# Attention and expert layers on one core: 64 units in one sequence, one batch's side work beside the other's units

## The chip, the cores and the metric

The kernel runs on one core of a Trainium2 chip. The metric is the device time of one execution in microseconds (us); the median of three runs is the figure before. The data are float32; inside, some operands are kept in bfloat16 (bf16), often as a value split into two or three bf16 parts whose sum is the float32 value.

## The reference

Input x is 2 batches of 1024 tokens of 128 numbers. All is computed in float32. LN is a layer norm without weights.

```python
x = x + LN(attention_1(LN(x)))     # 16 heads of 8; a bias table added to the logits
z = LN(x)
z = z + attention_2(LN(z) * ln1_w + ln1_b)   # 16 heads, no bias, then times w_proj
z = z + experts(LN(z) * ln2_w + ln2_b)       # each token goes to the one expert of 8
x = x + LN(z)                                # with the largest gate logit
```

attention_1 has `logits = q k^T / sqrt(8) + bias[h, i - j]`, softmax over 1024 keys per batch and head, and its result is normed and added to x. attention_2 has the same 1024 x 1024 logits per batch and head, without a bias. An expert is 128 -> 512, gelu, -> 128.

## The kernel before, in words

**Units and stages.** One head of one batch is a unit (1024 x 1024 logits). Stage 0 (attention_1) has 32 units, stage 1 (attention_2) has 32. The order inside a stage is head by head, and batch 0 then batch 1 within a head. Each engine's program is written out by hand in this order; semaphores tie the engines together. No scheduler changes it.

**What a unit does.** Its logits are computed twice. First in 8 "A blocks" (128 queries x 1024 keys): PE writes a block with `scores_a` (L1147) into one of two PSUM slots `SA`, and DVE takes each query's maximum over it, in stage 0 with the bias table added on the way (`block_max`, L876), in stage 1 with a plain reduce (L879). Then POOL splits the 8 maxima into three bf16 parts (`split_maxima`, L598 to L603), PE transposes them (L1184), ACT copies them out (L724), and SP sends them through DRAM into three extra rows of q (`maxima_of`, L424 and L428). Second in 8 "kb steps" of 128 keys x 1024 queries: PE writes two halves with `scores_b` (L1200), in stage 0 adds the bias by `bias_b` (L1207) from a skewed bf16 table, ACT takes the exponential (L737), and PE multiplies by v with `weigh_v` (L1155), two steps behind. At kb 2 ACT copies the last unit's sums out (`evacuate`, L707), and SP stores them. Three PSUM banks `SB` hold the halves on their way to ACT.

**Interleaving.** PE runs the kb steps of unit u together with the A blocks of unit u + 2: `scores_b`, `scores_a`, `scores_b`, `scores_a`, then `bias_b`, then `weigh_v`. An A block waits until DVE is done with the block two before.

**Loads.** SP loads, per head, the head's q and k rows for both batches (`rows_of`, 10 DMAs of 2048-token rows, issued over two units; L395, L398, L400), the bias table of the head (`table_of`, two DMAs of 480 KB, L332) and the skewed table (`skew_of`, 378 KB, L338). POOL copies v of the head for both batches (`v_of`, L579).

**Around the stages.** Before stage 0: x is normed (`norm_stats` L796 and L799, `norm_apply` L804 to L810, ACT's share L665 and L669), transposed (L1092), projected to q, k, v (L1113, L1116, L1121), split into parts (ACT L676 to L685, DVE L843 and L847) and stored to DRAM (L371, L375). Between the stages, for both batches at once: the last sums are loaded back, turned to token order (`to_natural`, L1138 and L1141), divided (`natural`, L860 and L863), normed, added to x, normed twice more, transposed, projected, split, stored, and rows of the first head are loaded. `keep_warm` (L1086) issues 12 idle matmuls. After stage 1: the same turn and division, times w_proj (L1299), added (L941), normed, the gate (L1330), the sorting of tokens by expert, 23 tiles of experts with indirect DMAs by POOL (L642, L653), the last norm and the stores.

## Time and profile before

| what | value |
|---|---|
| median of 3 runs | 986.47 us (985.25 to 987.48) |
| the profiled execution's own time | 982.59 us |
| its span, first to last instruction | 980.9 us |
| mean granted TensorE clock | 0.923 |
| busy PE, DVE, ACT, POOL | 830.7, 750.7, 648.3, 136.7 us |
| by stretch: up to the first kb step of stage 0 | 72.66 us |
| units 0 to 29 of stage 0 | 381.08 us |
| the last two units of stage 0 (no A blocks beside them) | 24.76 us |
| between the stages | 72.84 us |
| first unit of stage 1, then the other 31 | 12.73 and 287.03 us |
| after stage 1 | 129.80 us |

PE, DVE, ACT, POOL are TensorE, VectorE, ScalarE and GpSimd; SP issues DMAs. PEld is PE's load of the stationary operand. A busy share is an average over stretches with different limits, so the stretches are read apart. A matmul of float32 operands has two records.

### The profile page before, as it was taken

How to read it: one execution, taken by the hardware profiler on the slowest of the kernel's cores; microseconds unless marked ns; L12 is line 12 of the kernel's file. 1: busy time of each engine (PE TensorE's matmuls, PEld its weight loads, DVE VectorE, ACT ScalarE, POOL GpSimd, SP SyncE). 2: the span in 40 equal slices, each digit the busy share in tenths (PEclk: the TensorE clock that was granted, in tenths of full speed). 3: DMA queues.
4: the chain of work that ended last, by engine and by line, in shares of the span. 5: the costliest groups of instructions: out<-in, count | busy, mean ns of one | idle time of the engine just before them, and what ended most of it. 6: DMA issues, size and time to landing. Idle time of an engine off the chain costs nothing.

```text
span 980.9 us, 22683 instructions
## 1 busy us (share of the span) xinstructions
PE 830.7 (85%) x9011; PEld 315.4 (32%) x9011; DVE 750.7 (77%) x1211; ACT 648.3 (66%) x1272; POOL 136.7 (14%) x376
## 2 busy tenths in 40 slices
PE   2449999999999999999735799999999999974770
PEld 1203333333333333333312122222222222354760
DVE  6477777777777777774297899999999999266544
ACT  5406777677777777777434499999999999710222
POOL 8100000000000000000010011011010110003772
PEclk9758999999999999999967599999999999975995
DMA  2654434444444443330005365322222121010123
GB/s 62 173 157 104 120 95 109 105 106 107 107 98 110 107 106 93 87 86 16 16 1 152 81 149 134 105 69 70 65 66 70 58 69 42 24 44 19 50 49 94
DMA packets 55609, 82.79 MB, mean 84 GB/s; under 512 B 12336, under 2 KB 42480, under 8 KB 55504
## 3 DMA queue, kind: packets, MB, share of 16 engines
q1 hardware_dynamic: 53648, 76.57, 29.6%
q0 software_dynamic: 1472, 3.02, 1.3%
q10 hardware_dynamic: 384, 1.76, 0.6%
q8 instruction: 71, 1.16, 0.5%
q14 instruction: 34, 0.28, 0.1%
HBM read 62.31 MB, written 19.01 MB: 83 GB/s over the span
## 4 chain that ended last, share of the span: by engine, by line
PE 65%; ACT 9%; DVE 7%; POOL 4%; issue 4%; DMA 2%; SPq 1%; DVEq 0%; POOLq 0%
PE bank L1155 22%; PE bank L1200 17%; PE bank L1207 14%; PE bank L1147 8%; ACT prob_mem L737 8%; POOL moe_out L653 2%; POOL prob_mem L642 2%; DVE stats L796 1%; DVE norm L810 1%; DVE unit_max L879 1%; PE bank L1362 1%; DMA prob_mem<-tokens,gather_u 1%; DVE meanvar L799 1%; PE bank L1372 1%; DMA k_parts<-prob_mem 0%
## 5 line engine op out<-in xcount | busy, mean ns | idle before, releaser
L737 ACT ACTIVATE prob_mem<-bank 128x512 f32<-128x512 f32 x1024 | 556.1, 597 | 137.8 <-PE bank L1207 120.3
L876 DVE CUSTOM_DVE_ANT_0 y_res<-bank,tables 128x1024 bf16<-128x1024 f32 x256 | 312.3, 1224 | 99.5 <-PE bank L1147 94.3
L1155 PE MATMUL bank<-prob_mem,v_ring 128*32 128x256 f32 x4096 | 320.2, 387 | 4.6 <-issue 2.6
L879 DVE TENSOR_REDUCE unit_max<-bank 128x1 f32<-128x1024 f32 x256 | 293.2, 1216 | 13.8 <-PE bank L1147 10.7
L1147 PE MATMUL bank<-k_rows,q_rows 56*128 56x512 bf16 x512 | 161.2, 418 | 44.6 <-DMA k_rows<-k_parts 30.2
L1200 PE MATMUL bank<-q_rows,k_rows 59*128 59x512 bf16 x512 | 164.2, 391 | 2.3 <-ACT prob_mem L737 0.7
L1200 PE MATMUL bank<-more_rows 59*128 59x512 bf16 x512 | 158.9, 383 | 3.1 <-ACT prob_mem L737 1.1
L1147 PE MATMUL bank<-more_rows 56*128 56x512 bf16 x512 | 159.0, 382 | 0.0
L1207 PE MATMUL bank<-feat,flip 96*32 96x512 bf16 x2048 | 158.8, 387 | 0.0
L1155 PEld LDWEIGHTS bank<-prob_mem,v_ring 128*32 128x32 f32 x4096 | 102.2, 109 | 159.8 <-ACT prob_mem L737 72.9
L598 POOL CAST max_parts<-unit_max 128x8 bf16<-128x8 f32 x64 | 12.1, 189 | 689.7 <-DVE unit_max L876 386.1
L1200 PEld LDWEIGHTS bank<-more_rows 59*128 59x128 bf16 x512 | 40.2, 93 | 120.1 <-issue 60.1
L1200 PEld LDWEIGHTS bank<-q_rows,k_rows 59*128 59x128 bf16 x512 | 39.8, 93 | 118.3 <-issue 59.5
L773 ACT ACTIVATE prob_mem<-bank 128x512 f32<-128x512 f32 x23 | 13.7, 597 | 67.0 <-PE bank L1362 67.0
L1147 PEld LDWEIGHTS bank<-k_rows,q_rows 56*128 56x128 bf16 x512 | 37.2, 94 | 61.9 <-issue 22.5
L1207 PEld LDWEIGHTS bank<-feat,flip 96*32 96x32 bf16 x2048 | 30.9, 94 | 78.1 <-issue 78.1
L724 ACT COPY max_rows<-bank 24x128 bf16<-24x128 bf16 x64 | 15.9, 248 | 48.0 <-PE bank L1184 48.0
L860 DVE RECIPROCAL recip<-bank 128x64 f32<-128x64 f32 x8 | 4.4, 548 | 47.0 <-PE bank L1141 47.0
L1147 PEld LDWEIGHTS bank<-more_rows 56*128 56x128 bf16 x512 | 38.6, 93 | 0.0
L642 POOL DMA_INDIRECT prob_mem<-tokens,gather_u x23 | 24.8, 1080 | 64.2 <-DVE gather_u L1001 57.5
L665 ACT ACTIVATE std<-meanvar,eps_col 128x16 f32<-128x16 f32 x6 | 1.8, 308 | 46.9 <-DVE meanvar L799 46.9
L707 ACT COPY o_ring<-bank 128x256 f32<-128x256 f32 x64 | 24.4, 381 | 6.1 <-PE bank L1155 6.1
(160 smaller groups left out, 571.5 us busy)
## 6 DMA issues: line engine op xcount, KB each, us to landing
tables<-bias_rows SPq DMA_DIRECT2D x30, 480.0 KB, 5.3
unit_sums<-o_ring SPq DMA_DIRECT2D x64, 128.0 KB, 1.7
more_rows<-q_parts SPq DMA_DIRECT2D x64, 96.0 KB
more_rows<-k_parts SPq DMA_DIRECT2D x32, 192.0 KB
q_rows<-q_parts SPq DMA_DIRECT2D x56, 96.0 KB
k_rows<-k_parts SPq DMA_DIRECT2D x28, 192.0 KB
feat<-bias_parts SPq DMA_DIRECT2D x14, 378.0 KB, 3.8
w_moe<-in_L_ffn_w_dram SPq DMA_DIRECT2D x16, 256.0 KB, 3.8
```

What stands on the lines that cost most here:

```text
L642: nc.gpsimd.indirect_dma_start(out=slot_rows[:, j % 4, :], out_offset=None, in_=tokens_dram, in_offset=bass.IndirectOffsetOnAxis(ap=gather ...
L653: nc.gpsimd.indirect_dma_start(out=moe_dram, out_offset=bass.IndirectOffsetOnAxis(ap=token_u[:, j:j + 1], axis=0), in_=slot_y[:, j, :], in ...
L707: nc.scalar.copy(o_ring[:, slot, :], AV).then_inc(o_ready[a], 1)
L724: nc.scalar.copy(max_rows[:, slot, :], src).then_inc(max_copied[a], 1)
L737: nc.scalar.activation(prob[:, kb, half * N:(half + 1) * N], b_bank(entry(ul, kb, half)), ACT.Exp).then_inc(exp_done[a], 1)
L773: nc.scalar.activation(hidden[:, n % 2, :, :], bank[:, 2 + n % 2, :].rearrange("p (c n) -> p c n", c=HC), ACT.Gelu_apprx_tanh).then_inc(ge ...
L876: nc.vector.tensor_tensor_reduce(out=no_use[qb % 2], in0=scores, in1=bias, scale=1.0, scalar=LEAST, op0=ALU.add, op1=ALU.max, accum_out=un ...
L879: nc.vector.tensor_reduce(unit_max[:, slot, qb:qb + 1], scores, AX.X, ALU.max).then_inc(max_done[1], 1)
L1147: return nc.tensor.matmul(SA[slot][:, f, :], q_ring[head_slot][rows, b * L + qb * P:b * L + (qb + 1) * P], k_ring[head_slot][rows, b * L + ...
L1155: ins = nc.tensor.matmul(AV[VM * c:VM * (c + 1), :], v_ring[:, head_slot, b * QB + kb, :], prob[:, kb, c * W:(c + 1) * W], start=(kb == 0) ...
L1200: return nc.tensor.matmul(b_bank(entry(ul, kb, f)), k_ring[ul // B][rows, b * L + kb * P:b * L + (kb + 1) * P], q_ring[ul // B][rows, b * ...
L1207: ins = nc.tensor.matmul(b_bank(entry(ul, kb, f))[32 * c:32 * (c + 1), :], flip[:], skew[0:96, (ul // B) % 2, at:at + N], start=False, sto ...
```

## The change

**One sequence.** All 64 units stand in one list n = 0 to 63: stage, then batch, then head. Units 0 to 15 are stage 0 of batch 0, 16 to 31 stage 0 of batch 1, 32 to 47 and 48 to 63 the same for stage 1. The kb steps of unit n run with the A blocks of unit n + 2 through all stages; the part between the stages is gone.

**Side work.** What lay around the stages is cut by batch. Batch 0's first norm, projections and splits come before unit 0. The rest is put beside units by `beside(n, kb)`: after a kb step of n, PE does one side block in an `SA` slot, and the list `ring_order` gives A blocks and side blocks their slots in turn. There are 22 side blocks. Starting at n = 1: turn, qk, v, qk of batch 1 of stage 0 (n = 5 and 6). Starting at 17: two natural, turn, qk, v, qk, which make stage 1's batch 0. At 33 the same six for stage 1's batch 1. At 49: natural twice, turn, proj, turn, gate of batch 0. ACT copies turn, qk and v out of PSUM (`turn_out` L784 to L789, `qk_out` L798 and L799, `v_out` L808); DVE does natural (L917, L919), the additions (L925, L949) and, between its A blocks, the statistics of the norms (L858, L864: eight sets of 8 tiles inside the sequence). POOL now does the norms themselves (`normalise`: L587, L588 with a power of -0.5, eight L594), the addition to x (L657) and the split into parts (`split_parts`: L646 to L652, four operations on 128 x 512 for each of 4 pieces, two pieces in a unit). SP stores the parts (8 DMAs over two units).

**Loads.** q and k rows, tables and skewed tables are loaded for each unit, not for each head: 10 row DMAs of 1024 tokens a unit, one table DMA of 960 KB a unit, issued by ACT after the exponentials of kb 0 behind a wait for the maxima of unit n + 1, and one skew load a unit on SP, now issued ahead of the store of sums. There are 8 row slots, 3 skew slots, 2 table slots.

**Tail.** After unit 63 only batch 1 is turned, projected, normed and gated; `keep_warm` is gone. The last sums are loaded by 5 DMAs after the last unit. The last norm's 1/sqrt is POOL's, DVE does 10 tiles and ACT 6. The -1 rows of k are written once by DMA instead of POOL's fills.

The core of the diff (a line of "..." marks what is left out):

```diff
-    SUM_LOADS = 5 + 2 * 4
+    SUM_LOADS = 5
-    UB = 8
+    LEAD = 4
+    SLOTS = 8
...
+            for k, first in enumerate(FIRST):
+                p = n - first
+                if k and p == 0 and kb in (3, 6):
+                    return "natural", 2 * (k - 1) + (kb == 6)
+                if p == 4 and kb == 6:
+                    return "turn", k
+                if p == 5 and kb == 1:
+                    return "qk", 2 * k
+                if p == 5 and kb == 3:
+                    return "v", k
+                if p == 5 and kb == 5:
+                    return "qk", 2 * k + 1
+            p = n - LATE
...
+        ring_order = [("block", QB * m + qb) for m in range(2) for qb in range(QB)]
+        for n in range(NU):
+            for kb in range(QB):
+                if n + 2 < NU:
+                    ring_order.append(("block", QB * (n + 2) + kb))
+                if beside(n, kb):
+                    ring_order.append(beside(n, kb))
...
-        def table_of(queue, h, slot, half):
-            row = bias_dram[bass.ds(h, 1), half * HP:half * HP + TAW]
-            src = bass.AP(row.tensor, row.offset, [[1, HP], [1, TAW]])
-            queue.dma_start(bias_tab[half * HP:(half + 1) * HP, slot, :], src).then_inc(tab_loaded[slot], 16)
+        def table_of(queue, n):
+            row = bias_dram[head_of(n):head_of(n) + 1, 0:TAW]
+            src = bass.AP(row.tensor, row.offset, [[1, P], [1, TAW]])
+            queue.dma_start(bias_tab[:, n % 2, :], src).then_inc(tab_loaded[n % 2], 16)
...
-                    for ul in range(UB):
-                        u = UB * i + ul
-                        hl = ul // B
-                        if a == 0 and not (last and hl >= 2):
-                            if ul % B == 0:
-                                sp.wait_ge(max_done[0], QB * (u + B))
-                            table_of(sp, 4 * i + hl + 2, hl % 2, ul % B)
-                        if not (first and ul == 0):
-                            store_sums(a, u - 1, (ul - 1) % B)
-                        if not (last and ul == UB - 1):
-                            maxima_of(a, u + 1, ul + 1)
-                        if last and ul in (2, 3):
-                            load_sums(a, ul - 2, 0, H - UB // B)
-                        if last and ul >= 2:
-                            load_sums(a, ul % B, (u - 2) // B, 1)
-                        if a == 0 and ul % B == 0 and not (first and ul == 0) and not (last and hl == 3):
-                            sp.wait_ge(sb_done[0], 2 * QB * u)
-                            skew_of(sp, 4 * i + hl + 1, (hl + 1) % 2)
-                        if first and ul < B:
-                                sp.wait_ge(sb_done[a], 2 * QB * u)
-                            rows_of(a, 4 * i + hl + 3, (hl + 3) % 4, qk_loaded[a][(hl + 3) % 4], which=(ul % B,))
+            for n in range(NU):
+                if n + 2 < U:
+                    if n:
+                        sp.wait_ge(sb_done, 2 * QB * n)
+                    skew_of(sp, n + 2)
+                if n:
+                    store_sums(n - 1)
+                if n + 1 < NU:
+                    maxima_of(n + 1)
...
+                for k, first in enumerate(FIRST):
+                    if n == first + 7:
+                        store_parts(k + 1, 0)
+                    if n == first + 8:
+                        store_parts(k + 1, 1)
+                if n + LEAD < NU:
+                    if n + LEAD >= SLOTS:
+                        sp.wait_ge(sb_done, 2 * QB * (n + LEAD - SLOTS + 1))
+                    rows_of(n + LEAD)
...
-                def body(i, first=False, last=False):
-                    for ul in range(UB):
-                        if ul % 2 == 0:
-                            v_of(a, 4 * i + ul // 2, (ul // 2) % 2, not (first and ul < 4))
-                        if not (last and ul >= UB - AU):
-                            split_maxima(a, UB * i + ul + AU, ul % 2)
+            def normalise(k, b, src, dst):
+                rstd_of(k, b)
+                pool.wait_ge(ln_rstd, k + 1)
+                for t in range(b * TB, (b + 1) * TB):
+                    nc.gpsimd.tensor_scalar(dst[:, t, :], src[:, t, :], meanvar[:, t, 0:1], rstd[:, t:t + 1],
+                                            ALU.subtract, ALU.mult).then_inc(ln_done[k], 1)
...
+                nc.gpsimd.tensor_copy(hi, full).then_inc(part_step, 1)
+                pool.wait_ge(part_step, step + 1)
+                nc.gpsimd.tensor_tensor(full, full, hi, ALU.subtract).then_inc(part_step, 1)
+                pool.wait_ge(part_step, step + 2)
+                nc.gpsimd.tensor_copy(mid, full).then_inc(part_step, 1)
+                pool.wait_ge(part_step, step + 3)
+                nc.gpsimd.tensor_tensor(lo, full, mid, ALU.subtract).then_inc(part_lo, 1)
...
+            for n in range(NU):
+                if n + 1 < NU:
+                    split_maxima(n + 1)
+                    v_of(n + 1)
+                for k, first in enumerate(FIRST):
+                    p = n - first
+                    if k and p == 1:
+                        normalise(3 * k - 1, k - 1, norm, norm)
+                        add_to_x(3 * k - 1, k - 1)
+                    if k and p == 3:
+                        normalise(3 * k, k - 1, x_res, y_res)
+                    if p == 4:
+                        if k:
+                            normalise(3 * k + 1, k - 1, y_res, norm)
+                        else:
+                            normalise(1, 1, x_res, norm)
+                    if p in (6, 7):
+                        for s in range(2):
+                            split_parts(k + 1, p - 6, s)
...
+                    if kb == 0 and n + 3 < U:
+                        act.wait_ge(max_done, QB * (n + 2))
+                        table_of(act, n + 3)
+                    if kb == MAX_AT and n + 1 < NU:
+                        maxima_out(n + 1, max_t(out_entry(n)))
+                    kind, k = beside(n, kb) or (None, 0)
+                    if kind == "turn":
+                        turn_out(k)
+                    if kind == "qk":
+                        qk_out(k)
+                    if kind == "v":
+                        v_out(k)
...
+                                stats_of(3 * j - 1, b, 3 * kb, min(3 * kb + 3, TB), norm)
+                            if kb == 3:
+                                aggr_of(3 * j - 1, b, 0, TB)
+                        if j and p == 2:
+                            if kb == 3:
+                                dve.wait_ge(x_added, 2 * j)
+                            if 3 <= kb < 6:
+                                stats_of(3 * j, b, 3 * kb - 9, min(3 * kb - 6, TB), x_res)
+                            if kb == 6:
+                                aggr_of(3 * j, b, 0, TB)
...
-            pe.wait_ge(natural_done[0], G)
-            norm_group_out(pe, 2, G - 1)
-            keep_warm(WARM)
-            transposes(1, norm, lambda g: norm_group_out(pe, 3, g))
-            pe.wait_ge(weights_loaded, 16 * 8)
-            projections(1, w_qkv_sb[:, 0, :], w_qkv_sb[:, 1, :], w_qkv_sb[:, 2, :])
-            pe.wait_ge(part_rest[1], 2 * G)
-            pe.wait_ge(v_evac[1], G)
+                    what = beside(n, kb)
+                    if what:
+                        beside_block(what[0], what[1])
```

**ACT, stage 0, one unit and the step to the next.** L737 and L820 are the exponentials, L707 and L768 the copy of the sums, L724 and L775 that of the maxima. Before:

```order
L737 ACTIVATE prob_mem<-bank 128x512 x14
L707 COPY o_ring<-bank 128x256
L737 ACTIVATE prob_mem<-bank 128x512 x2
L724 COPY max_rows<-bank 24x128
```

Now, from unit 21 (kb 3) to unit 22 (kb 3), where the side work of stage 1's batch 0 stands:

```order
L820 ACTIVATE prob_mem<-bank 128x512 x8
L789 ACTIVATE prob_mem<-bank,ln_par 128x512 x2
L820 ACTIVATE prob_mem<-bank 128x512 x4
L392 DMA w_moe<-bias_rows 128x1920
L820 ACTIVATE prob_mem<-bank 128x512 x2
L798 ACTIVATE prob_mem<-bank 128x512
L799 COPY prob_mem<-bank 128x512
L768 COPY o_ring<-bank 128x256
L820 ACTIVATE prob_mem<-bank 128x512 x2
L775 COPY max_rows<-bank 24x128
L820 ACTIVATE prob_mem<-bank 128x512 x2
L808 COPY v_nat<-bank 128x512 x2
```

The copies of turn, qk and v, and the table's DMA (its tile has the name of the buffer it lies in), stand between exponentials.

**DVE, stage 1.** Before, the stage is one row, `L879 TENSOR_REDUCE unit_max<-bank 128x1 x256`. Now, in the A blocks of units 35 and 36:

```order
L912 TENSOR_REDUCE unit_max<-bank 128x1 x3
L917 RECIPROCAL recip<-bank 128x64
L919 TENSOR_TENSOR norm<-bank,recip 128x512
L912 TENSOR_REDUCE unit_max<-bank 128x1 x2
L858 BN_STATS stats<-norm 128x6 x3
L912 TENSOR_REDUCE unit_max<-bank 128x1
L858 BN_STATS stats<-norm 128x6 x3
L912 TENSOR_REDUCE unit_max<-bank 128x1
L858 BN_STATS stats<-norm 128x6 x2
L912 TENSOR_REDUCE unit_max<-bank 128x1
L864 BN_AGGR meanvar<-stats 128x2 x8
```

Division and statistics of a norm stand between the maxima of one unit's blocks.

**POOL, the split of parts (n = 39, 40).** L630 is the first of four operations on the maxima, L622 the copy of v:

```order
L622 COPY v_ring<-v_nat 128x8x8
L646 CAST prob_mem<-prob_mem 128x512
L648 TENSOR_TENSOR prob_mem<-prob_mem 128x512
L650 CAST prob_mem<-prob_mem 128x512
L652 TENSOR_TENSOR prob_mem<-prob_mem 128x512
L646 CAST prob_mem<-prob_mem 128x512
L648 TENSOR_TENSOR prob_mem<-prob_mem 128x512
L650 CAST prob_mem<-prob_mem 128x512
L652 TENSOR_TENSOR prob_mem<-prob_mem 128x512
L630 CAST max_parts<-unit_max 128x8
L632 TENSOR_TENSOR max_parts<-unit_max,max_parts 128x8
```

Eight operations that ACT and DVE had between the stages now stand on POOL ahead of the next unit's maxima.

## Rows read from the trace of the kernel before

**Rows 1.** Windows, one for each stretch: us, busy (count) by engine, clock, DMA

```profile
0.00:72.66 72.66, 27.68 (x116) 12.89 (x117) 44.88 (x100) 25.04 (x34) 26.86 (x42) 0.77 0.48 132
72.66:453.74 381.08, 376.50 (x4817) 134.79 (x4815) 297.23 (x483) 271.57 (x539) 25.99 (x135) 0.99 0.40 100
453.74:478.50 24.76, 23.79 (x293) 8.69 (x289) 0.52 (x2) 18.58 (x37) 0.98 (x5) 1.00 0.06 17
478.50:551.34 72.84, 33.24 (x157) 15.87 (x158) 57.82 (x175) 22.81 (x47) 4.36 (x6) 0.67 0.25 71
551.34:564.07 12.73, 12.47 (x83) 2.34 (x81) 10.48 (x10) 8.65 (x17) 0.98 (x5) 0.62 0.19 58
564.07:851.10 287.03, 281.87 (x2978) 74.01 (x2974) 266.25 (x233) 276.86 (x558) 25.85 (x135) 1.00 0.28 78
851.10:980.90 129.80, 75.15 (x580) 66.77 (x580) 73.55 (x212) 24.79 (x43) 51.74 (x48) 0.80 0.19 50
```

**Rows 2.** Timeline, stage 0, ACT: start, length, engine, line, tile [idle before]

```profile
202.35 1.09 ACT L737 ACTIVATE prob_mem<-bank 128x512 f32<-128x512 f32 x2 [0.43 <-PE bank L1207]
```

**Rows 3.** Timeline, stage 1, DVE and ACT

```profile
649.54 12.94 DVE L879 TENSOR_REDUCE unit_max<-bank 128x1 f32<-128x1024 f32 x11
...
652.86 6.63 ACT L737 ACTIVATE prob_mem<-bank 128x512 f32<-128x512 f32 x12 [0.17 <-PE bank L1200]
```

**Rows 4.** Timeline, before unit 0: SP's first row loads, the next store, PE

```profile
41.40 0.95 SPq L395 DMA_DIRECT2D q_rows<-q_parts  x2
...
46.14 0.57 SPq L371 DMA_DIRECT2D q_parts<-prob_mem  x1
...
51.62 1.04 PE L1147 MATMUL bank<-k_rows,q_rows 56*128 56x512 bf16 x4 [15.00 <-DMA k_rows<-k_parts]
```

**Rows 5.** Timeline between the stages, PE

```profile
478.53 0.41 PE L1138 MATMUL bank<-ident,prob_mem 16*128 16x16 f32 x4 [0.54 <-ACT prob_mem L737]
...
479.46 0.42 PE L1138 MATMUL bank<-ident,prob_mem 16*128 16x16 f32 x4
...
511.61 0.42 PEld L1092 LDWEIGHTS bank<-ident,norm 128*128 128x128 f32 x4 [0.35 <-DVE norm L810]
...
516.64 1.02 PE L1113 MATMUL bank<-feat,w_qkv_sb 128*128 128x512 f32 x2
...
518.36 1.05 PE L1121 MATMUL bank<-w_qkv_sb,feat 128*128 128x128 f32 x8
```

**Rows 6.** Timeline between the stages, DVE

```profile
489.56 0.54 DVE L860 RECIPROCAL recip<-bank 128x64 f32<-128x64 f32 x1
...
490.86 0.87 DVE L796 BATCH_NORM_STATS2 stats<-norm 128x6 f32<-128x128 f32 x4
...
497.88 3.18 DVE L796 BATCH_NORM_STATS2 stats<-x_res 128x6 f32<-128x128 f32 x16
...
500.98 1.14 DVE L799 BATCH_NORM_AGGREGATE meanvar<-stats 128x2 f32<-128x6 f32 x16
```

**Rows 7.** Groups by form, ACT: count, busy us, mean ns, idle before

```profile
L681 ACT COPY v_nat<-bank 128x512 f32<-128x512 f32 x8 | 4.7, 588 | 0.6 <-PE bank L1121 0.6
L764 ACT ACTIVATE feat<-bank,ln_par 128x512 f32<-128x512 f32 x2 | 1.5, 769 | 0.0
```

**Rows 8.** POOL: timeline of the bias split, first and last; group

```profile
32.03 0.61 POOL L584 CAST prob_mem<-prob_mem 128x512 bf16<-128x512 f32 x1 [7.14 <-DVE prob_mem L851]
...
34.98 1.48 POOL L590 TENSOR_TENSOR prob_mem<-prob_mem 128x512 bf16<-128x512 f32 x1
...
L630 POOL TENSOR_TENSOR x_res<-x_res,norm 128x512 f32<-128x512 f32 x2 | 3.6, 1827 | 39.9 <-DVE norm L810 39.9
```

**Rows 9.** DMA issues: KB each, median us from issue to landing

```profile
tables<-bias_rows SPq DMA_DIRECT2D x30, 480.0 KB, 5.3
...
tables<-bias_rows ACTq DMA_DIRECT2D x2, 480.0 KB, 8.4
```

**Rows 10.** Timeline after stage 1, the gate

```profile
875.62 4.21 PE L1330 MATMUL bank<-gate_w_sb,feat 128*128 128x8 f32 x32
```

More of the change, by code:

```diff
@@ L259, in sandwich_kernel @@
+        gate_feat = [sem(f"gate_feat{g}") for g in range(2)]
         gate_step = sem("gate_step")
@@ L325, in max_t, with entry @@
[L325 to L336 removed]
+        def entry(n, kb, f):
+            return n * EU + 2 * kb + f + (kb > MAX_AT)
@@ new lines, in split_parts @@
+            def split_parts(k, gi, s):
+                cols = slice(gi * N, (gi + 1) * N)
+                full = rest[:, gi, s, :]
+                hi, mid, lo = (parts[:, s, t, cols] for t in range(3))
+                step = 3 * (4 * (k - 1) + 2 * gi + s)
+                pool.wait_ge(qk_copied, 4 * (k - 1) + 2 * gi + s + 1)
+                if gi == 0 and s == 0:
+                    pool.wait_ge(parts_stored, 16 * 8 * k)
+                nc.gpsimd.tensor_copy(hi, full).then_inc(part_step, 1)
[5 more added lines that the diff above has]
+                nc.gpsimd.tensor_tensor(lo, full, mid, ALU.subtract).then_inc(part_lo, 1)
@@ L767, in four_tiles @@
-            def four_tiles(i, first=False, tiles=4):
-                for n in range(tiles):
-                    j = 4 * i + n
-                    act.wait_ge(up_mm, j + 1)
-                    if not (first and n < 2):
-                        act.wait_ge(down_mm, j - 1)
-                    nc.scalar.activation(hidden[:, n % 2, :, :], bank[:, 2 + n % 2, :].rearrange("p (c n) -> p c n", c=HC),
-                                         ACT.Gelu_apprx_tanh).then_inc(gelu_done, 1)
-            four_tiles(0, first=True)
@@ L777, in _ @@
-            for i in range(1, BODIES - 1):
-                four_tiles(i)
-            four_tiles(BODIES - 1, tiles=LAST)
-            norm_part(5, y_res, norm)
+            for gi in range(2):
+                cols = slice(gi * N, (gi + 1) * N)
+                act.wait_ge(first_q, gi + 1)
+                nc.scalar.activation(parts[:, 0, 0, cols], bank[:, 4 + 2 * gi, :], ACT.Copy, scale=SCALE).then_inc(part_hi, 1)
+                act.wait_ge(first_k, gi + 1)
+                nc.scalar.copy(parts[:, 1, 0, cols], bank[:, 5 + 2 * gi, :]).then_inc(part_hi, 1)
+                for s in range(2):
+                    act.wait_ge(part_rest, 2 * gi + s + 1)
+                    nc.scalar.copy(parts[:, s, 1, cols], rest[:, gi, s, :]).then_inc(part_mid, 1)
@@ new lines, in _ @@
+            evacuate(NU - 1)
+            act.wait_ge(gate_tp, 1)
+            nc.scalar.activation(feat[:, 2 * N:3 * N], bank[:, 2, :], ACT.Identity, scale=ln_par[:, 2:3],
+                                 bias=ln_par[:, 3:4]).then_inc(gate_feat[0], 1)
+            for j in range(NS):
+                act.wait_ge(up_mm, j + 1)
+                if j >= 2:
+                    act.wait_ge(down_mm, j - 1)
+                nc.scalar.activation(hidden[:, j % 2, :, :], bank[:, 2 + j % 2, :].rearrange("p (c n) -> p c n", c=HC),
+                                     ACT.Gelu_apprx_tanh).then_inc(gelu_done, 1)
@@ L1075, in _ @@
+            for g in range(G):
+                dve.wait_ge(ln_done[10 + g // 2], TB)
+                nc.vector.tensor_tensor(norm[:, group(g), :], x_res[:, group(g), :], norm[:, group(g), :], ALU.add).then_inc(out_ready, 1)
         @block.tensor
@@ new lines, in times @@
+            def times(rows, first_tile, weight, dst, width):
+                for tt in range(TG):
+                    ins = nc.tensor.matmul(dst[:, tt * width:(tt + 1) * width], rows[:, (first_tile + tt) * P:(first_tile + tt + 1) * P],
+                                           weight, start=True, stop=True)
+                return ins
+            pe.wait_ge(ln_done[0], TB)
+            for gi in range(2):
+                turn(norm, gi * TG, bank[:, gi, :]).then_inc(first_tp, 1)
+            pe.wait_ge(w_t_ready, 1)
@@ new lines, in _, with scores_a @@
+            ins.then_inc(bias_mm, 1)
+            for gi in range(2):
+                times(feat_b, gi * TG, w_in_t[:, 1, :], bank[:, gi, :], D).then_inc(first_v, 1)
+            def scores_a(m, qb, f):
+                rows = slice(f * HP, f * HP + KR)
+                place = ring_slot(("block", QB * m + qb))
+                return nc.tensor.matmul(place[:, f, :], q_rows[rows, m % SLOTS, qb * P:(qb + 1) * P],
+                                        k_rows[rows, m % SLOTS, f * N:(f + 1) * N], start=True, stop=True)
@@ L1317, in _ @@
[L1317 to L1330 removed]
+                ins.then_inc(sb_done, 1)
@@ L1331, in _ @@
+            pe.wait_ge(ln_done[9], TB)
+            pe.wait_ge(proj_added, 4)
+            for gi in range(2):
+                turn(norm, TB + gi * TG, bank[:, 2 + gi, :]).then_inc(gate_tp, 1)
+            for gi in range(2):
+                pe.wait_ge(gate_feat[gi], 1)
+                ins = times(feat, TB + gi * TG, gate_w_sb[:], bank[:, 7, gi * TG * E:(gi + 1) * TG * E], E)
             ins.then_inc(gate_mm, 1)
```

1356 lines of the change are left out of this document (650 added, 706 removed).

## The prediction

> **What bounds the kernel now.** I read the windows by stretch first [rows 1], since an average over the span hides that the stretches have different limits. In stage 0, PE is busy 376.5 of 381.1 us (99%), DVE 78%, ACT 71%: PE is the bound, and a unit takes 381.1 / 30 = 12.70 us, a kb step some 1.5. In stage 1, PE is at 98%, ACT at 96% and DVE at 93% of 287.0 us, and a unit takes 287.0 / 31 = 9.26 us. Between the stages lie 72.8 us in which no engine is full (PE 33, DVE 58, ACT 23) and the granted clock is 0.67. The timelines show how tight each stage is. In stage 0, ACT does its two exponentials in 1.09 us and waits 0.43 us for PE [rows 2]: there is room. In stage 1, twelve exponentials stand in 6.63 us and eleven maxima in 12.94 us with no gap [rows 3]: an exponential every 0.55, a maximum every 1.17 at most. ACT has 16 x 0.55 plus two small copies, DVE 8 x 1.15, both about 9.2 us of a 9.26 us unit. So work put beside stage 1 is hardly hidden on either of them.
>
> **Between the stages.** 72.8 us go [rows 1]. The last two units of stage 0 now have A blocks beside them: 2 x 12.70 for 24.8, +0.6. Stage 1's first unit no longer starts at the low clock (0.62): 9.26 for 12.73, -3.5. Sum **-75.7 us**.
>
> **Before unit 0.** SP began the first row loads at 41.4 us and was done at 46.1; PE started at 51.6 and its first kb step came at 72.7 [rows 4, 1]. Half of the tokens means 8 norm tiles for 16, two groups for four, and no POOL fills of k rows on the way. No row gives the new start; I estimate it by parts of the 41.4 us: half of x is normed by 10, the exponentials of the bias, which are not halved, end near 16, the parts of both groups follow by 24 and all stores by 28. So the first row loads start near 28.5, take the same 4.7 us, and land with some 4 us: PE starts near 37. Two units of A blocks take 18.4 us; the first piece of maxima and the skewed table, behind bias stores and the rows of unit 2 on SP, arrive at about the same moment. First kb step at 56.5, **-16 us** (bounds -11 to -20).
>
> **Beside stage 0** (10 side blocks; PE is the bound, so PE's own time counts). Four transposes take 0.42 us, so a turn 0.84; q and k of one group take 518.36 - 516.64 = 1.72; v of four tiles at most 1.05, of which about 0.15 is latency, so eight 1.8; a natural group 479.46 - 478.53 = 0.93 [rows 5]. Two turns, four qk, two v, two naturals: 1.7 + 6.9 + 3.6 + 1.9 = 14.1 us. ACT's copies are 0.59 each, 0.77 with a weight [rows 7], two per block; ACT's 0.43 us plus the time PE is away hide them, bar some 0.2 us per block. DVE's statistics are 0.20 us a tile and 0.07 for the aggregate [rows 6], 2.2 us a set, four sets. The second slot lets DVE be about a block late, so of a set some 0.3 us reaches PE. **+17 us** (bounds 14, PE alone, to 27, with all of DVE's and half of ACT's added). The table's DMA is issued on ACT; an issue takes 0.5 to 0.6 us, as SP's ten in 4.7 do [rows 4], just within the idle 0.43 us and slack of one bank: nothing. If that cover fails, 29 x 0.3 = 9 us.
>
> **Beside stage 1** (12 side blocks, four sets). ACT is never idle, so a block costs what ACT loses from its last exponential to the next. PE's block starts about when ACT has 0.55 us of exponentials left. Turn: PE 0.84 plus 0.2 latency, less 0.55, plus copies 1.54: 2.1. The qk and v blocks: 1.72 + 0.2 - 0.55 + 1.2 = 2.5 each. Natural: DVE's reciprocal and multiply are 490.86 - 489.56 = 1.30 [rows 6], plus 0.25 waiting for PE: 1.55. Proj: about 1.1 of waiting on PE and two additions of 0.7: 2.5. Gate: 1.7. So the six at n = 33: 2 x 1.55 + 2.1 + 3 x 2.5 = 12.7; the six at 49: 3.1 + 1.8 (plain copies) + 2.5 + 2.1 + 1.7 = 11.2; four sets of statistics, 2.2 each on a DVE with no spare time: 8.8. **+33 us** (bounds: 20, if DVE's and ACT's extras overlap each other, to 45, if each block costs one more 1.1 us step).
>
> **POOL.** A split of one piece is four operations; the same four on the bias ran from 32.03 to 34.98 + 1.48, 4.43 us [rows 8]. Two pieces, the maxima and v make 10 us in a unit: it fits in 12.7, not in 9.26, so in units 39 and 40 the maxima of the next unit come 0.8 and then 1.6 us late, against about 1.2 us that they have. The norm on POOL has no row in the trace. Its nearest are two-input operations on 128 x 512, 1.48 to 1.83 us; a quarter of the columns gives 0.37 to 0.46, and if all of it were fixed cost, 1.83. I take 0.4 a tile, 3.2 us a norm, because the columns must count for something: the four small operations of `split_maxima` fit between two blocks. The one place that then shows is n = 34, where statistics, norm and addition end some 13.5 us after the unit's start, 2 us into the next. **+2 us** (0 to 30). The Trainium skill, "GPSIMD Engine Reference" § 4.1 Engine selection, speaks against this move: elementwise work belongs on VectorE, since GpSimd is about twice as slow with two inputs, though near line rate with one. The row agrees for two inputs (1.83 us against 0.7 for DVE's multiply of the same shape). By the one-input part a tile would cost GpSimd about what it costs DVE in the statistics, an estimate of 0.3 us and 2.4 a norm, and the sum would be lower by under a microsecond.
>
> **Loads and SP.** Per unit SP issues 10 row DMAs (4.7 us [rows 4]) and some 2 us of others with one round trip to DRAM: 8 of 12.7 us in stage 0, just under 9.26 in stage 1, rows two units ahead. The store of parts adds 2.5 us in six units, behind the rows' lead: nothing. Tables and skew double, 0.65 MB more a unit. The 16 DMA engines were 40% busy at 100 GB/s [rows 1], 5.1 us for 1.27 MB; now some 8 us of 12.7. A table has from 2 us after a unit's start to the next unit's first block, 10.6 us, to land; 480 KB took 5.3 us [rows 9], 960 KB then some 7.6. Nothing.
>
> **Tail.** The gate takes 4.21 us for 32 records [rows 10], now half; the norms before it, half of the statistics aggregate and half the tiles but without ACT's help, save about 2; the last norm's root is partly hidden, 1. Against it: five load DMAs for two after the last unit, whole batches before a turn, and a low clock without `keep_warm`. **-4 us** (-9 to +2).
>
> **Sum.** -75.7 - 16 + 17 + 33 + 2 - 4 = -43.7 us, from 982.6 us, the profiled execution's own time, to 938.9. The median of the runs is 3.9 us above that execution, so I forecast **943 us**. Differences under 0.2% (2 us) can't be told from none here.
>
> **Rivals.**
> *A, the table comes late (slower).* Place: DVE's first block of each unit in stage 0. Two tables issued together on ACT's queue took 8.4 us for 480 KB each [rows 9]. If a 960 KB table took twice that, 16.8 us, it would be 6.2 us late in 29 units, +180 us, 1120 us. It decides from a landing of 10.6 us, and the gain is eaten at 12.1 (43.7 / 29 = 1.5 more). For it: the load is doubled and skew and rows of the same unit share the way. Against: 40% busy leaves room. Chance 0.08. The Trainium skill, "DMA: Bandwidth & Descriptors" § Issuing engines are not separate DMA queues, says that a DMA issued elsewhere still runs on the same 16 engines; moving the table to ACT's queue then buys no transfer time, and what ACT saves is SP's issue alone.
> *B, POOL is late.* At 0.8 us a tile (between 0.4 and 1.83) DVE's statistics, PE's turns and the maxima behind the norms wait, in both stages, 1 to 4 us at seven places, some +17: 960 us. Chance 0.15.
> *C, side work hides better.* If only the fullest engine's own time counts (14 and 20), with a start at -18: 924 us. Against: two slots and three banks hold little. Chance 0.13.
> *D, the sequence stalls at the change of stage or a load,* so that half of the 72.8 us comes back: 975 us. Nothing in the order speaks for it; rows of unit 32 are loaded at n = 28. Chance 0.04.
>
> **Numbers.** Forecast case 0.60, its own range 930 to 956. With B's and C's sides the range for 8 in 10 is 925 to 968. Slower takes A, 0.08; the same 0.02; faster the rest, 0.90.
>
> **What would show it.** First kb step at 55 to 59 us, the last near 811; stage 0 units without side work still 12.7 us, stage 1's 9.26; units 5, 6, 17 to 22 longer by 17 us in all, 33 to 37 and 49 to 53 by 33; no wait of DVE's A blocks for `bias_rows`; PE's granted clock at full without a break through the stages. Wrong if units without side blocks have grown (A), if waits for POOL's norms or splits exceed 5 us in all (B), or if DVE or ACT are idle for more than 3 us at a side block.

## The result, and the profile of the changed kernel

The changed kernel takes 978.39 us (median of 8 runs, 976.09 to 982.32) beside 985.62 us for the kernel before in the same session: ratio 0.9926, 95% interval 0.9911 to 0.9941. In a second session it was 0.9951 (0.9934 to 0.9969). So it is faster, but by 7 us where 43.7 were forecast; 978 lies above the range of 925 to 968. The profiled execution took 976.09 us, with a span of 974.3.

Windows by stretch of the changed kernel, as in [rows 1]: up to the first kb step, the 32 units of stage 0, the 32 of stage 1, the tail (columns: us, busy time and count by engine, granted clock, DMA share, GB/s).

```profile
0.00:56.43 56.43, 20.82 (x84) 7.91 (x85) 30.29 (x68) 15.10 (x17) 15.74 (x42) 0.72 0.51 149
56.43:486.53 430.10, 418.80 (x5216) 152.70 (x5217) 325.43 (x568) 298.45 (x591) 92.81 (x234) 0.99 0.48 150
486.53:839.46 352.93, 323.98 (x3187) 92.27 (x3183) 291.29 (x316) 294.27 (x589) 77.80 (x213) 0.96 0.25 72
839.46:974.30 134.84, 70.17 (x504) 64.38 (x504) 62.56 (x183) 18.51 (x32) 57.59 (x54) 0.74 0.18 48
```

Against the forecast, stretch by stretch (us of span; "forecast" is the row of before plus the terms of the prediction):

| stretch | before | forecast | change |
|---|---|---|---|
| before the first kb step | 72.7 | 56.7 | 56.4 |
| stage 0, 32 units | 405.8 | 423.4 | 430.1 |
| between the stages | 72.8 | 0 | 0 |
| stage 1, 32 units | 299.8 | 329.3, and POOL 2 | 352.9 |
| tail | 129.8 | 125.8 | 134.8 |

The gap between the stages is gone and the start is 16 us earlier, as forecast. 28 us are lost beside the units, 21.6 of them in stage 1, where the clock of 0.96 is already a sign, and 9 in the tail. PE's waits between the first kb step and the last exponential say who. L1192 transposes the split maxima, L1223 is the natural block, L1162 is `scores_a`, L1208 `scores_b`, L1129 the turn block (engine, line, releaser: us in total, times, longest):

```profile
PE bank L1192 <- POOL max_parts L635: 11.1, 3, 5.0
PE bank L1223 <- DMA prob_mem<-unit_sums: 7.9, 3, 3.3
...
PE bank L1162 <- DVE unit_max L912: 3.6, 5, 2.9
PE bank L1208 <- DMA q_rows<-maxima_rows: 3.5, 2, 3.1
PE bank L1129 <- POOL norm L594: 2.5, 2, 1.5
```

The first is PE waiting for the maxima of the next unit, which POOL splits only after a norm. Timeline of POOL from unit 34 into unit 35, where the norm, then the addition to x, stand ahead of the split of the maxima of unit 36, whose A blocks ran beside unit 34:

```profile
517.45 0.25 POOL L587 TENSOR_SCALAR rstd<-meanvar 128x8 f32<-128x8 f32 x1 [5.56 <-DVE meanvar L864]
517.79 1.67 POOL L588 TENSOR_TENSOR rstd<-rstd,halves 128x8 f32<-128x8 f32 x1
519.56 6.25 POOL L594 TENSOR_SCALAR norm<-norm,meanvar,rstd 128x128 f32<-128x128 f32 x8
525.89 2.48 POOL L657 TENSOR_TENSOR x_res<-x_res,norm 128x512 f32<-128x512 f32 x2
528.32 0.19 POOL L630 CAST max_parts<-unit_max 128x8 bf16<-128x8 f32 x1
```

Eight tiles take 6.25 us, 0.78 each, where the forecast took 0.4; the power before them takes 1.67. A norm is 8.4 us of POOL, with the addition 10.9, and stage 1's unit is 9.26. DVE's maxima beside it:

```profile
517.27 7.98 DVE L912 TENSOR_REDUCE unit_max<-bank 128x1 f32<-128x1024 f32 x7
```

The first four of the seven are the last of unit 36 and ended at 521.86 (the other three belong to unit 37), so the split came 6.5 us late. PE:

```profile
529.38 0.27 PE L1192 MATMUL bank<-ident_b,max_parts 128*24 128x128 bf16 x1 [4.98 <-POOL max_parts L635]
529.58 0.60 PE L1208 MATMUL bank<-q_rows,k_rows 59*128 59x512 bf16 x1
```

A matmul on 512 columns that takes 0.38 to 0.39 us elsewhere takes 0.60 behind the wait. The windows of the same place show why: the granted clock falls to 0.50, the lower of its two levels (1.2 GHz), after PE's pause.

```profile
519.50:528.30 8.80, 4.79 (x52) 1.20 (x48) 5.75 (x6) 4.78 (x10) 8.66 (x10) 0.88 0.29 88
528.30:533.00 4.70, 3.62 (x25) 0.76 (x25) 2.15 (x5) 2.15 (x5) 0.95 (x6) 0.50 0.06 16
533.00:540.00 7.00, 6.81 (x70) 1.70 (x64) 7.00 (x19) 5.87 (x11) 1.00 (x6) 1.00 0.46 134
```

The second wait is at units 17, 33 and 49, the natural blocks. SP's queue ahead of unit 17 (L441 to L447 are the row loads of unit 20, L476 and L479 the sums), and PE:

```profile
276.19 0.55 SPq L458 DMA_DIRECT2D q_rows<-maxima_rows  x2
276.77 0.94 SPq L441 DMA_DIRECT2D q_rows<-q_parts  x2
...
280.97 0.48 SPq L447 DMA_DIRECT2D k_rows<-k_parts  x1
281.55 2.47 SPq L476 DMA_DIRECT2D prob_mem<-unit_sums  x4
284.07 0.61 SPq L479 DMA_DIRECT2D prob_mem<-unit_sums  x1
```

```profile
290.26 0.39 PE L1223 MATMUL bank<-ident,prob_mem 16*128 16x16 f32 x4 [3.33 <-DMA prob_mem<-unit_sums]
```

The sums are issued behind ten row loads that are first needed beside unit 18. SP's order is behind the one long wait for `maxima_rows` as well, 3.1 us at unit 42. The copy of these maxima and their store (SPq is SP issuing a DMA):

```profile
604.26 0.25 ACT L775 COPY max_rows<-bank 24x128 bf16<-24x128 bf16 x1
```

```profile
608.58 0.40 SPq L454 DMA_DIRECT2D maxima_rows<-max_rows  x1
```

From 598.94 to 608.0 SP issued four stores of parts, ten row loads and two loads of expert weights. POOL's split of parts, which the expectations below name for these 3.1 us, held no maxima up: POOL waited 0.8 us for DVE ahead of each split of maxima at units 39 and 40. Theory 1 is then: the loss is POOL's and SP's lateness, at seven or eight places. Rival 2: the side work itself costs more than forecast on full engines, and the waits only show where.

### The profile page after: what moved, and what is told of

The parts are those of the page before. It is cut to its first block, busy times and chain, and to the rows that moved or that the text cites. A ratio compares the mean times of both kernels' runs of the same rounds, so it can differ in the third digit from the quotient of the medians.

```text
span 974.3 us, 22607 instructions
## 1 busy us (share of the span) xinstructions
PE 833.8 (86%) x8987; PEld 317.3 (33%) x8987; DVE 709.6 (73%) x1133; ACT 626.3 (64%) x1227; POOL 243.9 (25%) x543
## 4 chain that ended last, share of the span: by engine, by line
PE 58%; DVE 11%; POOL 9%; DMA 5%; SPq 5%; ACT 5%; issue 4%; another core or an unknown queue 1%; POOLq 0%; DVEq 0%; ACTq 0%
PE bank L1183 18%; PE bank L1208 14%; PE bank L1215 11%; PE bank L1162 7%; ACT prob_mem L820 4%; POOL norm L594 3%; DVE no_use L909 3%; DVE unit_max L912 3%; DVE stats L858 2%; PE bank L1374 2%; PE bank L1365 2%; POOL rstd L588 2%; DMA prob_mem<-unit_sums 2%; PE bank L1134 1%; POOL y_res L594 1%
## 5 line engine op out<-in xcount | busy, mean ns | idle before, releaser
L820 ACT ACTIVATE prob_mem<-bank 128x512 f32<-128x512 f32 x1024 | 557.2, 599 | 164.1 <-PE bank L1215 123.5
L909 DVE CUSTOM_DVE_ANT_0 no_use<-bank,w_moe 128x1024 bf16<-128x1024 f32 x256 | 311.6, 1223 | 109.8 <-PE bank L1162 109.7
L1162 PE MATMUL bank<-k_rows,q_rows 56*128 56x512 bf16 x1024 | 320.3, 398 | 29.3 <-DMA k_rows<-k_parts 18.0
L1208 PE MATMUL bank<-q_rows,k_rows 59*128 59x512 bf16 x1024 | 329.4, 391 | 7.3 <-DMA q_rows<-maxima_rows 3.5
L630 POOL CAST max_parts<-unit_max 128x8 bf16<-128x8 f32 x64 | 12.2, 191 | 589.5 <-DVE unit_max L909 327.5
L1215 PE MATMUL bank<-skew_mem,flip 96*32 96x512 bf16 x2048 | 159.6, 389 | 0.0
L1208 PEld LDWEIGHTS bank<-q_rows,k_rows 59*128 59x128 bf16 x1024 | 80.6, 94 | 239.2 <-issue 125.2
L1162 PEld LDWEIGHTS bank<-k_rows,q_rows 56*128 56x128 bf16 x1024 | 76.0, 94 | 41.9 <-issue 19.3
L1215 PEld LDWEIGHTS bank<-skew_mem,flip 96*32 96x32 bf16 x2048 | 31.0, 95 | 81.6 <-issue 81.6
L775 ACT COPY max_rows<-bank 24x128 bf16<-24x128 bf16 x64 | 16.0, 250 | 39.3 <-PE bank L1192 39.3
L1374 PE MATMUL bank<-prob_mem 128*128 128x128 f32 x184 | 27.4, 298 | 6.6 <-ACT prob_mem L844 3.5
L917 DVE RECIPROCAL recip<-bank 128x64 f32<-128x64 f32 x8 | 4.5, 558 | 38.0 <-PE bank L1226 38.0
L1365 PE MATMUL bank<-prob_mem 128*128 128x128 f32 x184 | 28.3, 303 | 1.8 <-issue 1.7
L722 POOL DMA_INDIRECT moe_out<-prob_mem,token_u x23 | 25.2, 1095 | 16.7 <-DVE prob_mem L1074 12.1
L1374 PEld LDWEIGHTS bank<-prob_mem 128*128 128x128 f32 x184 | 24.9, 210 | 7.3 <-ACT prob_mem L844 3.9
L1365 PEld LDWEIGHTS bank<-prob_mem 128*128 128x128 f32 x184 | 26.2, 219 | 2.6 <-issue 2.6
```

What stands on the lines that cost most here:

```text
L722: nc.gpsimd.indirect_dma_start(out=moe_dram, out_offset=bass.IndirectOffsetOnAxis(ap=token_u[:, j:j + 1], axis=0), in_=slot_y[:, j, :], in ...
L820: nc.scalar.activation(prob[:, kb, half * N:(half + 1) * N], b_bank(entry(n, kb, half)), ACT.Exp).then_inc(exp_done, 1)
L909: nc.vector.tensor_tensor_reduce(out=no_use[:, qb % 2, :], in0=scores, in1=bias, scale=1.0, scalar=LEAST, op0=ALU.add, op1=ALU.max, accum_ ...
L1162: return nc.tensor.matmul(place[:, f, :], q_rows[rows, m % SLOTS, qb * P:(qb + 1) * P], k_rows[rows, m % SLOTS, f * N:(f + 1) * N], start= ...
L1208: return nc.tensor.matmul(b_bank(entry(n, kb, f)), k_rows[rows, n % SLOTS, kb * P:(kb + 1) * P], q_rows[rows, n % SLOTS, f * N:(f + 1) * N ...
L1215: ins = nc.tensor.matmul(b_bank(entry(n, kb, f))[32 * c:32 * (c + 1), :], flip[:], skew[0:96, n % 3, at:at + N], start=False, stop=True, t ...
```

## The experiments

Each ratio is to the kernel before, run beside it.

**sums_first.** SP alone is reordered:

```diff
                 if n + 1 < NU:
                     maxima_of(n + 1)
+                if n in (H, 2 * H, 3 * H):
+                    load_sums(n // H - 1)
...
                     rows_of(n + LEAD)
-                if n in (H, 2 * H, 3 * H):
-                    load_sums(n // H - 1)
```

> Only SP's order changes: the five loads of the last sixteen units' sums stand ahead of the ten row loads of unit n + 4, not behind them. Theory 1: the time that the change lost against the forecast lies in waits, and 7.9 us of them (3.3, 2.0 and 2.6 at units 17, 33 and 49) are PE waiting at the natural block for sums that SP issued 4.7 us too late. Then these three waits are gone and the time is 978.4 - 7.9 = 970.5 us (969 to 973). Rival 2: the side work itself costs more on full engines than the forecast had; a wait taken away at one place comes back at the next, and the time stays within 2 us of 978.4.

Measured: 960.69 us, ratio 0.9794 (0.9781 to 0.9808), so 13 to 15 us under the change's ratio, for 7.9 us of waits, and more than theory 1's range. The three waits are gone from the trace. Rival 2 falls for this part; the surplus of 5 us and more is a question of its own (warm_natural, below).

**norm_few_columns.** POOL's tiles do 16 of 128 columns (`dst[:, t, 0:16]`, `src[:, t, 0:16]`):

> Each of POOL's norm tiles does 16 of its 128 columns (the other 112 are left as they are; two fills of norm and y_res are added on POOL before unit 0). The forecast took 0.4 us a tile, the profile of the change shows 0.78. If columns set it, a tile falls to some 0.15 to 0.25 us; if it is fixed cost it stays near 0.78 and nothing moves. Theory 1: of the waits behind POOL, 2.6 + 5.0 + 3.5 us (maxima held up by a norm) and 1.0 + 1.5 + 2.9 us (a norm that PE or DVE waits for) go, 16.5 us in all, and the 3.1 us behind the split of parts stay: 962 us (960 to 966). Rival 2 (side work itself costs it): 975 to 979.

Measured: 952.75 us, 0.9716 (0.9687 to 0.9744). POOL's group of it, then the same group of the change (count, busy us, mean ns):

```profile
L594 POOL TENSOR_SCALAR norm<-y_res,meanvar,rstd 128x16 f32<-128x16 f32 x24 | 9.9, 432 | 0.3
```

```profile
L594 POOL TENSOR_SCALAR norm<-y_res,meanvar,rstd 128x128 f32<-128x128 f32 x24 | 18.7, 795 | 0.3
```

A tile is 0.43 us with 16 columns and 0.79 with 128: by these two, 0.38 fixed and 0.0032 per column. So neither end of what was expected holds for the tile. The kernel leaves 112 of the columns out of the norms, so it shows a cost and is no version to use. The time went down by 21 to 23 us by ratio, more than the 16.5 us of waits and below theory 1's range, though one of the waits is still there with 2.0 us (for the maxima of unit 36). Rival 2 falls; what the surplus is stays open here.

**norms_on_dve.** The tiles go to DVE (`apply(k, b, ..., 4 * i, 4 * i + 4)` in two kb steps), POOL keeps the power and the addition:

> The tiles of all side norms go from POOL to DVE, four at a time in two kb steps (2.15 us a norm by the trace), POOL keeps the power and the addition, which moves to the next unit. Theory 1: POOL's lateness of 16.5 us goes; four of these norms stand in stage 1, where DVE has no idle time, and cost 4 x 2.15 = 8.6 us, four in stage 0 some 0.3 to 0.5 us each beyond what DVE has free: 978.4 - 16.5 + 8.6 + 1.5 = 972 us (969 to 975). Rival 2: DVE is the fuller engine, so it is slower than the change: 985 us or more.

Measured: 962.88 us, 0.9828 (0.9809 to 0.9848), 10 to 12 us better than the change, where 6 were expected. Rival 2 falls. Even on an engine with no idle time the tile, 0.27 us there (2.15 for eight), is cheaper than on POOL where a maximum waits behind it.

**tables_twice.** A second load of each table into unread memory:

> Every table DMA is issued twice, the second into memory that nobody reads; DVE waits for both. It adds 30.7 MB. Theory 1: loads are hidden by a wide margin in the change: landing goes from 5.6 to some 7 to 9 us, under the 10.6 us that a table has; ACT issues 29 more DMAs at 0.1 us or less of its time seen: 978 to 980 us. Rival 3 (the loads per unit take away the gain, through rows, skew or table late): the units of stage 0 grow by more than 0.3 us each, 988 us or more.

Measured: 1016.72 us, 1.0367 (1.0347 to 1.0387): 36 us over before, some 42 over the change by ratio. Theory 1 was wrong here, and so was the mechanism of rival 3. Tables landed in 7.5 us (median of both loads; the second alone 9.1), and both loads of every table were there at least 1.8 us before DVE's first block of its unit. What grew most is the round trip of the maxima through DRAM on SP. SP's wait for their store (us in total, times, longest), between 60 and 450 us, in the change:

```profile
SPq L458 <- DMA maxima_rows<-max_rows: 76.9, 29, 4.7
```

and here, with PE's wait for the rows behind it:

```profile
SPq L460 <- DMA maxima_rows<-max_rows: 148.3, 26, 7.5
```

```profile
PE bank L1210 <- DMA q_rows<-maxima_rows: 26.6, 16, 4.2
```

2.7 us a store became 5.7. PE's wait for the sums at unit 17 grew too, from 3.3 to 7.7 us; together these are 31 us of waits for the 42 lost. That the larger transfers on the same 16 engines hold the stores up is argued from these rows; no run moves the table's time to prove it.

**change_again.** The change itself, a second time.

> The change itself, unedited, as the measure for the runs beside it. Theory 1: 0.992 to 0.993 of the time before. Its first profile ended 133.7 us after the last copy of sums; four variants whose tail is the same code took 128.5 to 129.2. If those 5 us belong to the code, they are here again; if to that one execution, this profile shows some 128.8.

Measured: 975.67 us, 0.9951 (0.9934 to 0.9969). Its tail, from the last exponential on, and that of the change's first profile above:

```profile
845.42:974.20 128.78, 65.62 (x504) 59.36 (x504) 64.30 (x183) 18.70 (x33) 58.16 (x54) 0.77 0.19 50
```

So 6 of the tail's 9 lost us belong to one execution: in it ACT stands idle for 5.4 and 4.5 us between expert tiles, PE and POOL with it, with no releaser that the profile names. What they wait for stays open. PE's waits inside the stages are the same as in the first profile within 0.6 us a line, but the stages are 5 us longer: unit 17 (from one copy of sums, L768, to the next) is 20.8 us long here and was 19.4 there, for 12.54 of a plain unit and a wait of 3.4 and 3.3 us. At unit 33 PE's wait is 2.0 us in both; behind it the granted clock is 0.50 here and the unit 7.2 us over a plain one, 1.00 and 4.6 us there.

**pool_spaced.** The same operations on POOL in other units. PE's turn, qk and v blocks, DVE's statistics and SP's stores of parts move with them (left out below):

```diff
-                    if k and p == 1:
-                        normalise(3 * k - 1, k - 1, norm, norm)
-                        add_to_x(3 * k - 1, k - 1)
-                    if k and p == 3:
+                    if k and p == 1:
+                        rstd_of(3 * k - 1, k - 1)
+                    if k and p == 2:
+                        tiles_of_norm(3 * k - 1, k - 1, norm, norm)
+                    if k and p == 3:
+                        add_to_x(3 * k - 1, k - 1)
+                    if k and p == 4:
                         normalise(3 * k, k - 1, x_res, y_res)
...
-                    if p in (6, 7):
-                        for s in range(2):
-                            split_parts(k + 1, p - 6, s)
-                if n == LATE + 2:
+                    if 7 <= p <= 10:
+                        split_parts(k + 1, (p - 7) // 2, (p - 7) % 2)
+                if n == LATE + 3:
```

> The same work on POOL, in other units: the tiles of each norm stand at the start of a unit, behind its maxima, the addition to x in a unit of its own, the four split pieces one to a unit; turn, qk and v are two units later, the stores of parts two and three. Theory 1: the waits behind POOL (2.6 + 5.0 + 3.5 + 1.0 + 1.5 + 2.9 for norms, 3.1 for splits = 19.6 us) go and nothing is paid for it: 18 to 20 us under the change of the same call. Rival 2 (the pieces cost the same wherever they stand): within 3 us of it. Rival 4 (POOL's power and tiles fill a unit of stage 1 to 1.3 + 1.9 + 6.3 = 9.5 us, over its 9.26): only half is won, 10 us.

Measured: 950.07 us, 0.9690 (0.9667 to 0.9714): 25.6 us under the change of the same session. PE waits neither for POOL's maxima nor for its norms any more; the 7.9 us for sums are still there. The wait for a row of maxima at unit 42 is gone with the moved stores, but 2.7 us of the same kind now stand at unit 14. Rival 2 and rival 4 fall: the same work costs 25 us less where it holds nobody up.

**pool_spaced_sums.** Both edits.

> pool_spaced with the sums loaded ahead of the rows as in sums_first, which took 9.2 us out of the stages. Theory 1: the two causes are at different units and add up: 27 to 29 us under the change of the same call, so near the 943 us that were forecast. If they cover each other, as in rival 2, 20 us or less.

Measured: 935.68 us, 0.9550 (0.9537 to 0.9562), 40 us under the change. The two causes add up, and each is worth more than its waits. Its windows by stretch:

```profile
0.00:56.96 56.96, 22.10 (x85) 8.34 (x85) 30.23 (x68) 14.99 (x17) 15.55 (x42) 0.74 0.51 148
56.96:481.50 424.54, 417.90 (x5219) 152.60 (x5218) 325.32 (x568) 297.84 (x591) 92.66 (x234) 0.99 0.49 152
481.50:807.75 326.25, 317.13 (x3187) 92.44 (x3183) 290.10 (x316) 294.06 (x589) 77.47 (x213) 0.99 0.27 78
807.75:937.60 129.85, 66.55 (x504) 60.62 (x504) 63.93 (x183) 18.70 (x33) 58.20 (x54) 0.77 0.19 50
```

57.0, 424.5, 326.3 and 129.9 us stand against the forecast's 56.7, 423.4, 331.3 and 125.8. The side blocks, with their counts unchanged (x5219, x3187), cost about what was forecast.

**two_queues.** The last sums issued by SP and ACT:

> pool_spaced_sums, and the last loads of sums after unit 63 issued on two queues: two columns and the denominators on SP, two columns on ACT, which is idle there. Five issues of 0.62 us stand in a row ahead of the landing; with three in a row PE's wait of 7.4 us is 1.2 us shorter: 1 us under pool_spaced_sums. If the landing is set by the 16 DMA engines and not by the issues, no difference.

Measured: 934.24 us, 0.9527 (0.9513 to 0.9541). Its tail is no shorter: 130.44 us, and PE's wait 7.0 for 7.4.

```profile
802.36:932.80 130.44, 67.67 (x504) 61.33 (x504) 64.33 (x183) 18.69 (x32) 58.80 (x54) 0.76 0.18 49
```

The medians are 1.4 us apart and the intervals overlap. Of the profiled executions, this one's stages are 5.4 us shorter: 4.0 at units 13 and 14, where in the other SP issued the store of the maxima 5 us after their copy, behind stores of parts and ten row loads, and 1.5 at unit 53. So the edit gives nothing.

**warm_natural.** The change, with nine idle matmuls ahead of each wait for sums:

```diff
                 if kind == "natural":
+                    if k % 2 == 0:
+                        keep_warm(9, place[:, 0, :])
                     pe.wait_ge(sums_loaded, ...)
```

> The change with nine idle matmuls (1.9 us at the full clock) into the free slot ahead of each of PE's waits for sums at units 17, 33 and 49; nothing is loaded earlier. In the change's second profile these three waits are 3.4, 2.0 and 2.5 us long, yet their units are 8.2, 7.2 and 7.7 us longer than plain ones, against 1.9, 2.6 and 2.6 with the sums in time, and the granted clock is 0.50 behind the first. Theory 5: the rest is PE at its lower clock after the pause. Then the clock stays at 1.00, the units lose 1.9 + 3.4, 2.6 + 2.0 and 2.6 + 2.5 us, and the time is some 7 us under the change (0.986 to 0.989 of the time before). Rival 6 (the rest is the refilling of the slots and banks after the pause, whatever the clock): same as the change, 0.993 to 0.995, or slower.

Measured: 973.03 us, 0.9875 (0.9852 to 0.9897). Windows around unit 17's wait, in change_again, in the change's first profile, and then here:

```profile
288.00:292.00 4.00, 1.40 (x8) 1.21 (x8) 0.00 (x0) 0.00 (x0) 0.00 (x0) 0.78 0.49 111
292.00:296.00 4.00, 4.00 (x30) 0.86 (x32) 2.39 (x4) 1.08 (x2) 0.00 (x0) 0.50 0.27 80
```

```profile
292.00:296.00 4.00, 4.00 (x42) 1.19 (x40) 3.18 (x5) 1.83 (x4) 0.00 (x0) 0.74 0.31 85
```

```profile
288.00:292.00 4.00, 2.82 (x32) 1.41 (x32) 1.74 (x3) 0.89 (x2) 0.00 (x0) 1.00 0.15 42
292.00:296.00 4.00, 4.00 (x52) 1.77 (x48) 3.31 (x7) 2.37 (x5) 0.00 (x0) 1.00 0.38 108
```

52 matmuls in four us for 30 and 42, and units 17, 33 and 49, from copy to copy of sums, are 5.4, 4.6 and 5.0 us over plain ones (12.54 and 9.26), for 8.2, 7.2 and 7.7 in change_again: just the wait plus the natural blocks. Rival 6 falls. The surplus at these three waits is the clock; for the waits behind POOL it is argued from the windows at 519 to 540 us alone, since no run fills those pauses.

**warm_tail.** pool_spaced_sums with idle matmuls in the tail's two pauses:

> pool_spaced_sums with 30 idle matmuls ahead of PE's wait for the last sums (7.4 us long) and 28 ahead of its wait for the last norm before the gate (7.1 us), where the granted clock is 0.50. Theory 5: PE's 3.8, 2.2 and 5.1 us of transposes, projection and gate there run at twice the rate: 4 to 5 us under pool_spaced_sums (0.950 of the time before). Rival 6: under 1 us.

Measured: 935.55 us beside 985.14 for before, 0.9491 (0.9470 to 0.9512), the fastest version, 0.6% under pool_spaced_sums by ratio. The transposes of the last gate show the clock (idle before in brackets), in pool_spaced_sums and then here:

```profile
831.09 1.97 PE L1134 MATMUL bank<-ident,norm 128*128 128x128 f32 x8 [7.10 <-DVE norm L874]
```

```profile
825.61 1.09 PE L1134 MATMUL bank<-ident,norm 128*128 128x128 f32 x8 [1.06 <-DVE norm L874]
```

From the last copy of sums to the matmul behind the gate (`onehot`) it is 27.2 us in the profile, for 29.7 in pool_spaced_sums: 2.5 of the 4 to 5 us expected, since the clock is at 0.50 again from 828 us on, inside the gate's matmuls. The profiled tail is still 130.7 us, because it has unexplained idle stretches between expert tiles too, as the change's first profile (one of 4.3 us), so the profile doesn't confirm the rest.

## Why the prediction was wrong

- **Between the stages, -75.7, and before unit 0, -16:** right. The first kb step came at 56.43 us (55 to 59 forecast) and the table's issue on ACT cost no unit anything: plain units take 12.54 and 9.26 us. (A table landed in 5.6 us, where 7.6 were forecast. The 12.70 forecast for stage 0 was a mean that held the first unit's start and, at every eighth unit of before, 0.8 us more.)
- **Beside stage 0, +17, and beside stage 1, +33:** right as prices of the blocks. With POOL and SP out of the way the stages are 1.1 us over and 5.0 under their forecasts (pool_spaced_sums). That 1.1 is so small is in part luck: 32 plain units at 12.70 were 5.1 us too many, and the profile holds 4.0 us of a late row. Unit by unit in two_queues, which lacks that row, the blocks with the statistics add 16.7 and 29.2 us to plain units, for 17 and 33.
- **POOL, +2 (0 to 30):** this step failed. "I take 0.4 a tile ... because the columns must count for something" was measured at 0.79, inside its bounds, and the power, 0.25 + 1.67 us a norm, stood in no term. The prediction let statistics, norm and addition end 2 us into unit 35; norm and addition take 10.9 us, more than a unit of stage 1, and the maxima behind them were split 6.5 us late. The term is worth 25.6 us (pool_spaced). The splits of parts, named as 0.8 and 1.6 us late, were not: a piece took 3.7 us, not 4.43. Rival B had the mechanism and a tile of 0.8, but priced it at 17 us, and its sign, over 5 us of waits for norms, is what the first profile shows (16.5). On that choice the Trainium skill, "GPSIMD Engine Reference" § 4.1 Engine selection, has near line rate for one input; here POOL takes 0.79 us where DVE takes 0.27 for the same tile, so the measurement decides against it.
- **Loads and SP, 0:** the second step that failed. SP's time per unit was summed, and its order not read: the sums stand behind ten row loads. Worth 13 to 15 us (sums_first; 14.4 on top of pool_spaced). The store of parts, put at nothing behind the rows' lead, held up the maxima behind it for 3.1 us at unit 42. The case that a load stalls the sequence was rival D, at 0.04, with another place in mind; its 975 leaves out the 3.9 us of the median and should be 979, so that it meets the measured time is chance.
- **A pause of PE costs more than its length:** in no term and no rival. The waits of 28.6 us on PE in the stages stood for some 40. For the three waits for sums the clock is shown to be the surplus (warm_natural).
- **Tail, -4 (-9 to +2):** 128.8 us in change_again, so -1; the -4 was too good, since PE waits 7.4 us for five loads issued after the last unit. The first profile's +5 is inside no term.
- **Sum:** 943 + 25.6 + 14.4 = 983 us for 978.4 measured. The two terms are of the second session, in which the change stood at 0.9951, or 980.8 of 985.62 us. With both terms repaired in the code, 0.9550 of before was measured, where 943 is 0.956 of the 986.47 us before.
- **Rival A:** the table is never late in the change: every one landed at least 3.1 us before DVE's first block of its unit. But the margin of the loads is much smaller than the sum by DMA share said: 960 KB more a unit cost some 42 us, not through the table's deadline but for the most part through the maxima's round trip.

## What to carry to other kernels

Work moved to an idle engine is free only if nothing urgent is queued behind it: compare the whole piece, its small scalar operations too, with the slack of what stands next on that engine, and place it in a unit where it ends in time. Do the same for a queue's order, not only for its sum of issues. And price every new wait of PE at its length plus the slower matmuls behind it, or fill it.

## What was unexpected of the hardware

- POOL's power on 128 x 8 takes 1.67 us, eight times its subtraction on the same shape (0.20). A tensor_scalar with two per-partition scalars on 128 x 128 takes 0.79 us.
- PE's granted clock went to 0.50 after pauses of 3.4 and 5.0 us (and of 2.0 and 2.5 at units 33 and 49 in change_again, whose loss was cured alike by idle matmuls), and was back at 1.00 in the window from 533 us on, where PE had started again at 529.4. The same pause of 2.0 us left it at 1.00 in the change's first profile. The Trainium skill, "TensorE: Matmul & The Clock Gate" § HAM oscillation — how this bites in real kernels, tells of a kernel that falls to the lower clock at each wait for a DMA; the windows above agree for waits on a DMA and for one on POOL, though not every wait did it.
- SP's wait for a 6 KB store to land rose from 2.7 to 5.7 us when 30.7 MB of other loads were added over 32 units.
